# Scatter with the one-hot block as the stationary operand, in four 32-column groups

## What is computed

```python
h = relu(layernorm(x));  s = h[:, :32] @ W_up_s;  v = h[:, 32:] (as 32 x 3) @ W_up_v
w0, w1, w2, w3 = split(silu(silu(edge_feats @ A1 + b1) @ A2 + b2) @ A3, 4)
out_s0 = s[src] * y_s * w0            # y_s, y_v: columns 0 and 1..3 of edge_attr_4
out_s3 = sum_i v[src]_i * y_v_i / sqrt(3) * w3
out_v1 = s[src] * y_v * w1            # 3 components
out_v2 = v[src] * y_s * w2            # 3 components
message = segment_sum([out_s0, out_s3, out_v1, out_v2], dst) / 10
out = x + [message_s @ W_out_s, message_v @ W_out_v]
```

## Time and profile before

| | |
|---|---|
| median of three runs, without the profiler | 2046.74 us (2044.48 to 2048.28) |
| span of the profiled execution | 2586.7 us |
| TensorE matmuls busy | 2104.9 us (81% of the span) |
| weight loads busy | 1617.6 us (63%) |
| GpSimd (gathers) busy | 1577.2 us (61%) |
| VectorE busy | 928.9 us (36%) |
| ScalarE busy | 397.6 us (15%) |
| mean granted TensorE clock | 0.792 |
| DMA | 128.17 MB, mean 50 GB/s |

### The profile page before, as it was taken

One profiled execution on the slowest core, in us unless ns is written; L12 is line 12 of the kernel. 1 busy time (PEld: TensorE's weight loads), 2 busy tenths in 40 slices (PEclk: granted clock), 3 DMA queues, 4 the chain that ended last, 5 costly groups with the idle time before them and its releaser, 6 DMA issues.

```text
span 2586.7 us, 35524 instructions
## 1 busy us (share of the span) xinstructions
PE 2104.9 (81%) x10298; PEld 1617.6 (63%) x10298; DVE 928.9 (36%) x2228; ACT 397.6 (15%) x640; POOL 1577.2 (61%) x1627
## 2 busy tenths in 40 slices
PE   6477888878888889787878888888888878888878
PEld 4366666656666667566656666666666666666666
DVE  4233333333333333333333333333333334333334
ACT  3011111111111111111111111111111111111111
POOL 5666666566566566666666566656666656666661
PEclk8687788788778777877878788778788877778787
DMA  6111111111111111111111111111111111111111
GB/s 189 50 47 45 46 45 46 44 45 47 43 47 46 43 45 45 47 45 45 45 47 45 45 46 46 44 44 46 46 44 46 46 45 43 47 45 47 46 47 62
DMA packets 111056, 128.17 MB, mean 50 GB/s; under 512 B 70594, under 2 KB 83170, under 8 KB 110916
## 3 DMA queue, kind: packets, MB, share of 16 engines
q0 software_dynamic: 50336, 102.64, 15.2%
q1 hardware_dynamic: 60516, 25.37, 3.8%
q10 hardware_dynamic: 192, 0.02, 0.0%
HBM read 121.47 MB, written 6.43 MB: 49 GB/s over the span
## 4 chain that ended last, share of the span: by engine, by line
PE 62%; another core or an unknown queue 19%; issue 15%; ACT 2%; DVE 0%; ACTq 0%; DVEq 0%; DMA 0%; SPq 0%
PE pss L703 25%; PE psw L687 14%; PE pso L715 8%; PE ps L670 7%; PE ps L677 7%; ACT sums L542 1%; ACT h L524 1%; ACT h L529 0%; DVE msgs L613 0%; ACTq L541 0%; DVEq L621 0%; DMA ef_in<-in_efT 0%; ACTq L557 0%; SPq L453 0%
## 5 line engine op out<-in xcount | busy, mean ns | idle before, releaser
L498 POOL DMA_INDIRECT rows<-node_table,src_in x1563 | 1560.3, 998 | 943.5 <-DVE msgs L613 469.5
L703 PEld LDWEIGHTS pss<-onehot,msgs 128*128 128x128 f32 x6256 | 895.0, 217 | 554.8 <-issue 513.8
L703 PE MATMUL pss<-onehot,msgs 128*128 128x32 f32 (+1 forms) x6256 | 947.9, 301 | 246.8 <-issue 233.6
L611 DVE TENSOR_TENSOR msgs<-rows,psw 128x256 f32<-128x256 f32 x391 | 164.7, 421 | 1583.4 <-remote 905.3
L687 PE MATMUL psw<-a_bd,h 128*128 128x256 f32 x1564 | 527.9, 470 | 22.8 <-issue 11.7
L715 PE MATMUL pso<-sums,w_out 128*128 128x128 f32 x1568 | 282.5, 338 | 171.2 <-ACT sums L542 144.8
L687 PEld LDWEIGHTS psw<-a_bd,h 128*128 128x128 f32 x1564 | 339.2, 240 | 69.2 <-issue 21.7
L613 DVE TENSOR_TENSOR msgs<-rows,psw 128x768 f32<-128x768 f32 x391 | 370.6, 948 | 0.0
L715 PEld LDWEIGHTS pso<-sums,w_out 128*128 128x128 f32 x1568 | 251.9, 244 | 189.2 <-issue 187.7
L670 PE MATMUL ps<-ef_in,a_bd 16*128 16x512 f32 x392 | 257.6, 740 | 19.8 <-DMA ef_in<-in_efT 10.9
L524 ACT ACTIVATE h<-ps,b_sb 128x512 f32<-128x512 f32 x196 | 134.9, 688 | 824.9 <-remote 398.5
(11 more groups left out here) (55 smaller groups left out, 88.0 us busy)
## 6 DMA issues: line engine op xcount, KB each, us to landing
rows<-node_table,src_in POOLq DMA_INDIRECT x1563
ef_in<-in_efT SPq DMA_DIRECT2D x98, 64.0 KB
xT_sb<-in_xT SPq DMA_DIRECT2D x7, 448.0 KB, 8.3
x_sb<-in_x SPq DMA_DIRECT2D x7, 448.0 KB, 7.8
attr_in<-in_attr SPq DMA_DIRECT2D x98, 32.0 KB
out_T<-xT_sb SPq DMA_DIRECT2D x1, 3136.0 KB, 8.8
node_table<-tab_sb SPq DMA_DIRECT2D x7, 256.0 KB, 3.7
src_in<-in_src SPq DMA_DIRECT2D x98, 8.0 KB
```

The lines of the kernel that those rows point to most:

```text
L498: pool.indirect_dma_start(out=rows[:, QT * p + t, :], out_offset=None, in_=table, in_offset=bass.IndirectOffsetOnAxis(ap=src_in[:, b, at:a ...
L611: dve.tensor_tensor(m[:, :, :, 0, :], g[:, :, 0, :].unsqueeze(2).broadcast_to([P, QT, 2, MUL]), w[:, :, :, 0, :], ALU.mult)
L703: last = nc.tensor.matmul(pss[:, o % 2, 2 * q + i, c0:c1, :].rearrange("p c w -> p (c w)"), msgs[:, p % SLOTS, t, part, :], onehot[:, g % ...
```

## The change

`scatter` swaps its operands. The one-hot block of one tile and one attribute (128 edges x 32 nodes) is now stationary, and the messages are moved past it: 128 columns for attribute 0, twice 32 columns for each of attributes 1 to 3. Its output is 32 partitions (nodes) by 256 columns (features). The four tiles of a quad belong to four different windows, and each writes its own 32 partitions of `pss`. The host reorders the edges so that a quad holds one tile of each of four windows, and the next quad the other tile of each.

The sums of an oct then lie as 128 nodes x 256 features. `copy_sums` copies 256 columns instead of 512; a new step `turn` transposes them in two matmuls against an identity; a new ScalarE step `copy_turned` brings 256 columns back to SBUF; `project` needs two matmuls instead of four. `msgs` and `onehot` have four slots instead of two. `layer_1` and `layer_2` stand one per quad, two octs ahead. Windows are added six behind instead of eight. In the last pass all eight quads run (seven before), still with 27 gathers.

```diff
+OW = QT
+MSG_SLOTS = 4
+HOT_SLOTS = 4
-WINDOW_LAG = 2 * OW
+WINDOW_LAG = OW + 2
-OUT_WEIGHT_LOADS = 1 + 3 * 3
+OUT_WEIGHT_LOADS = 2 + 3 * 2
...
-        pss = pb("pss", [P, 2, OW, 4, W])
-        pso = pb("pso", [P, 2, 512])
+        pss = pb("pss", [P, 2, 512])
+        psx = pb("psx", [P, 2, 512])
+        pst = psx[:, 0, 0:CH]
+        pso = psx[:, 1, 0:OW * W]
...
+                pool.memset(identity[:, :], 0.0).then_inc(identity_built, 1)
+                pool.wait_ge(identity_built, 1)
+                pool.affine_select(out=identity[:, :], in_=identity[:, :], compare_op=ALU.not_equal, fill=1.0,
+                                   base=0, pattern=[[-1, P]], channel_multiplier=1).then_inc(identity_built, 1)
...
+                    def copy_sums(j, o):
+
+                        act.wait_ge(scatter_done, j * QB + 2 * o + 2 + SCATTER_CREDIT)
+                        act.wait_ge(sums_turned, j * OCTS + o + 1)
+                        act.activation(sums[:, o % 2, :], pss[:, o % 2, 0:CH], ACT.Copy).then_inc(sums_copied, 1)
+
+                    def copy_turned(j, o):
+
+                        act.wait_ge(sums_turned, j * OCTS + o + 1 + TURN_CREDIT)
                         act.wait_ge(out_ready, j * OCTS + o + 1)
+                        act.activation(sums_t[:, o % 2], pst.rearrange("p (k n) -> p k n", k=2),
+                                       ACT.Copy).then_inc(turned_copied, 1)
...
-                        for i in range(2):
-                            for part, c0, c1 in ((0, 0, 1), (1, 1, 4)):
-                                for t in (2 * i, 2 * i + 1):
-                                    last = nc.tensor.matmul(
-                                        pss[:, o % 2, 2 * q + i, c0:c1, :].rearrange("p c w -> p (c w)"),
-                                        msgs[:, p % SLOTS, t, part, :],
-                                        onehot[:, g % 2, QT * k + t, c0:c1, :].rearrange("p c w -> p (c w)"),
-                                        start=(t == 2 * i), stop=(t == 2 * i + 1))
+                        for c in range(4):
+                            for w in range(OW):
+                                m = msgs[:, p % MSG_SLOTS, w]
+                                acc = pss[W * w:W * (w + 1), o % 2, 0:CH]
+                                if c == 0:
+                                    moving, to = m[:, 0, :], acc[:, 0:F]
+                                else:
+                                    moving = m[:, 1, :].rearrange("p (k u) -> p k u", k=4)[:, 0:c + 1:c, :]
+                                    to = acc.rearrange("p (k u) -> p k u", k=8)[:, 3 + c:8:4 - c, :]
+                                last = nc.tensor.matmul(to, onehot[:, o, QT * half + w, c, :], moving,
+                                                        start=(half == 0 and c == 0), stop=(half == 1 and c == 3),
+                                                        skip_group_check=True)
                         last.then_inc(scatter_done, 1)
...
+                    def turn(j, o):
...
+                        for k in range(2):
+                            last = nc.tensor.transpose(pst[:, k * P:(k + 1) * P], sums[:, o % 2, k * P:(k + 1) * P],
+                                                       identity[:, :])
+                        last.then_inc(sums_turned, 1)
...
+                        for k in range(2):
+                            last = nc.tensor.matmul(pso, w_out[:, k, :], sums_t[:, o % 2, k, :],
+                                                    start=(k == 0), stop=(k == 1))
                         last.then_inc(out_ready, 1)
```

More of the change, by code:

```diff
@@ L78, in quad_tiles @@
 def quad_tiles(p):
-    return max(0, min(QT, LAST_TILES - QT * p))
+    o, half = divmod(p, 2)
+    begins = [o * OCT_EDGES + w * GROUP + half * P for w in range(OW)]
+    return sum(b < LAST_EDGES for b in begins)
 def gnn_layer_kernel(nc, x, xT, src, dst, dst_groups, attr, efT, Wus, Wuv, A1, b1, A2, b2, A3, Wos, Wov, outT):
@@ L554, in _ @@
-                    for part in range(4):
-                        silu(0, 0, part)
+                        for o in range(OCTS):
+                            ahead = (j, o + 2) if o + 2 < OCTS else (j + 1, o + 2 - OCTS)
+                            before = not (first and o == 0)
+                            if before:
+                                copy_sums(j, o - 1)
+                            if not (last and o + 2 >= OCTS):
+                                silu_1(*ahead)
+                            if before:
+                                copy_turned(j, o - 1)
+                            if not (last and o + 2 >= OCTS):
+                                silu_2(*ahead)
@@ L723, in iteration @@
                     def iteration(j, first=False, last=False):
-                        quads = LAST_QUADS if last else QB
-                        for p in range(quads):
-                            b, k = divmod(p, QUADS)
-                            if p + 1 < quads:
+                        for p in range(QB):
+                            o, half = divmod(p, 2)
+                            ahead = (j, o + 2) if o + 2 < OCTS else (j + 1, o + 2 - OCTS)
+                            if p + 1 < QB:
@@ L730, in iteration @@
                                 layer_3(j + 1, 0)
-                            if b == 0:
-                                mlp_part(j, 1, k)
-                            elif not last:
-                                mlp_part(j + 1, 0, k)
-                            ends = last and p == quads - 1
-                            if not ends:
-                                scatter(j, p)
-                            if p % 2 == 0 and not (first and p == 0):
-                                project(j, p // 2 - 1)
-                            if ends:
-                                scatter(j, p)
-                    for part in range(4):
-                        mlp_part(0, 0, part)
+                            if half == 1 and not (first and o == 0):
+                                project(j, o - 1)
+                            if not (last and o + 2 >= OCTS):
+                                (layer_1, layer_2)[half](*ahead)
+                            if half == 0 and not (first and o == 0):
+                                turn(j, o - 1)
+                            scatter(j, p)
+                    for o in range(2):
+                        layer_1(0, o)
+                    for o in range(2):
+                        layer_2(0, o)
                     layer_3(0, 0)
```

149 lines of the change are left out of this document (72 added, 77 removed).

## The result

Six runs of each kernel side by side gave a median of 2041.42 us after the change (2039.56 to 2045.56) against 2047.51 us before: ratio 0.9972, 95% interval 0.9961 to 0.9982. The forecast was no change, 2048.3 us.

What follows compares the result with a forecast made beforehand. The prediction took GpSimd's gathers as the bound before and after. Prologue -0.4 and tail +2.0, all other terms 0, gave +1.6 us on the median of 2046.7: 2048.3 us, range 2020 to 2090.

Steps and rivals of the forecast that it cites:

- the floor of 2016 us: Whole kernel: 1563 gathers starting every 1.25 us plus 19.5 us behind the last start; lengthened gathers add up to 80 us.
- That the stalls belong to profiling: TensorE in the profiled execution: idle stretches between matmuls, inferred from some 540 us of span existing only under the profiler.
- TensorE's room: TensorE per quad: 3.94 us of work against 5.00 us for four gathers, so 1.06 us to spare.
- messages start when gathers land: VectorE: one-hot multiplications keep their place against the gathers, lengthening keeps its size; value 0, bounds -30 and +50 us.
- rival B: Gathers: TensorE delays them in the metric too and a shorter scatter frees them; about 2020 us, chance 0.11.
- The tail, "+2.0 us": Last messages to store: scatter +0.3, turn +0.8, copy_turned +0.4, project -0.4, four windows instead of two +0.9; together +2.0 us.
- The 19.5 us of the floor: End of the kernel: time from the last gather's start through messages, scatter, projection, window and store to the span's end.
- Scatter, 2.15 us: TensorE, new scatter per quad: column groups one after the other, loads hidden, 2.15 us; bounds 0.54 and 3.55 us.
- estimate of 2.0 us from sequencer time: TensorE, new scatter: about 62 ns of sequencer time per MATMUL, counted on 32 pairs, 2.0 us per quad.
- Transposes: TensorE, projection: two transposes and two matmuls make 8 pairs per oct if a transpose splits like a product, again 0.92 us.
- Prologue, -0.4 us: Start of the kernel: two fewer w_out loads, up to -0.8 us, and two small GpSimd operations for the identity; taken as -0.4.
- Rival C: One-hot multiplication shifts against the gathers: 0.05 us in each of 196 octs is 10 us, 2038 or 2058 us; chance 0.13.

Runs made afterwards that it cites:

- the second profile: The kernel before, unchanged, profiled again: span 2046.5 us, in an execution that took 2048.32 us.
- after_layer3_twice: The kernel after with each layer_3 matmul issued twice, the second writing the same result: median 2045.64 us, ratio 0.9999 to the kernel before.
- after_one_group: The kernel after with all four windows of a quad written to partitions 0 to 31, one column group, sums wrong: 2041.63 us, ratio 0.9997 to the kernel before.
- before_four_slots: The kernel before with four slots of msgs and onehot instead of two, nothing else: ratio 0.9998 to the kernel before.
- before_half_scatter: The kernel before with the second tile of each window left out of the scatter, half the edges missing: median 2039.44 us, ratio 0.997.

## Why the prediction was wrong, point by point

**The bound: right.** The gathers bound both kernels, and the floor of 2016 us with up to 80 us of lengthened gathers on top describes both: the traces hold 1503.5 and 1500.0 us of gather work, of which 1563 x 0.944 = 1475 is the undisturbed pace, so 28 and 25 us of lengthening.

**"That the stalls belong to profiling": wrong.** They belonged to one execution; the second profile has no such stretch. I had marked this step as an inference. It cost nothing in the sum, since I left the stalls out of the metric, but with them I left out TensorE altogether.

**What failed: TensorE's room was reckoned at full clock only.** That took two terms of the sum with it. The forecast was +1.6 us and the two traces are 5.9 us apart the other way; of these 7.5 us, 3.5 lie in the gathers (forecast 0), 4.5 in the tail (forecast +2.0, measured -2.5), and 0.5 go the other way in the prologue.

**VectorE, "messages start when gathers land", value 0: failed.** It holds for 353 of 391 quads before, and for 384 of 392 after. I had compared TensorE's 3.94 us at full clock with 5.00 us and called the difference room. But half-clock stretches remain without the stalls (granted clock 0.50 from 180 to 190 us), and there the work of a quad takes nearly twice as long. In before, 22 of the 196 multiplications follow messages that had waited for TensorE, and the gathers beside these 22 carry 8.4 of the 28 us of lengthening; after has six such multiplications and 1.4 of 25 us. The lengthened gathers came out 3.5 us cheaper in all, not 0. That is rival B's cause (TensorE delays gathers in the metric too), with one difference. The gathers never wait for messages; they are lengthened. B priced all 30 us above the floor, 2020 us. Most of those 30 us come from the usual distance of 0.98 us, which the change doesn't touch: the gathers beside the other 174 multiplications carry 20 us. That late messages are the way holds for these two kernels; `after_layer3_twice` and `after_one_group` lose the gain by other ways (above).

**The tail, "+2.0 us": wrong in sign.** It measured -2.5 us (22.9 to 20.4 behind the start of the last gather). From the last messages to the store it was 10.8 us before and 7.6 after, not 2 us more. The 19.5 us of the floor were taken at full clock as well; they measured 22.9. I laid the new steps end to end behind the last messages and took all at full clock. In both traces part of the tail runs at half clock (granted clock 0.50 from 2028 to 2036 us before, and from 2016 to 2024 us after), and TensorE still has the scatter of the last quad but one and a projection to do when the last messages come. TensorE's tail before and after:

```profile
2024.92 2.03 PE L703 MATMUL pss<-onehot,msgs 128*128 128x32 f32 x16 [1.88 <-DVE msgs L613]
2027.64 2.04 PE L715 MATMUL pso<-sums,w_out 128*128 128x128 f32 x8 [0.69 <-ACT sums L542]
2029.47 3.57 PE L703 MATMUL pss<-onehot,msgs 128*128 128x32 f32 x16
2033.51 1.97 PE L715 MATMUL pso<-sums,w_out 128*128 128x64 f32 x8 [0.47 <-ACT sums L542]
```
```profile
2020.32 1.29 PE L736 MATMUL pss<-msgs,onehot 128*32 128x128 f32 x32 [0.79 <-DVE msgs L640]
2021.54 2.08 PE L714 MATMUL psw<-a_bd,h 128*128 128x256 f32 x4
2023.41 0.64 PE L746 MATMUL psx<-identity,sums 128*128 128x128 f32 x2
2023.97 1.12 PE L736 MATMUL pss<-msgs,onehot 128*32 128x128 f32 x32
2025.02 0.71 PE L755 MATMUL psx<-sums_t,w_out 128*128 128x128 f32 x4
2025.66 0.76 PE L736 MATMUL pss<-msgs,onehot 128*32 128x128 f32 x32
2026.92 0.44 PE L746 MATMUL psx<-identity,sums 128*128 128x128 f32 x2 [0.50 <-ACT sums L556]
2027.84 0.71 PE L755 MATMUL psx<-sums_t,w_out 128*128 128x128 f32 x4 [0.47 <-ACT sums_t L562]
```

The last scatter took 3.57 us before and 0.76 after, the last projection 1.97 and 0.71. `turn` took 0.5 us of the 0.8 given, `copy_turned` the 0.4. Something I had overlooked works against the gain: in the kernel after the last three tiles lie in two quads, where before they lay in one, so that there is one more pass of messages and scatter, and the last messages start 3.55 us behind the start of the last gather, against 2.87 before.

How much the tail gives hangs on where a half-clock stretch falls. `before_four_slots` has the last scatter at half clock too, 3.57 us, and 22.6 us of tail. In the two profiles of the kernel before with the multiplication first it took 1.92 and 2.02 us, and the tails are 19.9 and 19.5 us, no longer than the 19.5 to 20.4 of after and its variant with the same edit. So the 2.5 us belong to the lower clock as much as to the shorter scatter.

**Scatter, 2.15 us: the wrong end of the bounds.** It takes 0.6 to 0.8 us at full clock, close to the low bound of 0.54. The 2.15 us was right for the case that it described: one column group measured 2.24 to 2.33. The drain that the Trainium skill's "TensorEngine Tiling (Array Packing)", section Key Properties, names for a change of mode does not stand out: from the last narrow load at 1504.77 + 0.60 to the loads of `layer_3` at 1505.60 it is 0.23 us, against 0.17 to 0.24 us of idle time ahead of other groups of loads. The Trainium skill's same page and section say that different tiles can load weights and multiply in parallel; 0.83 against 2.33 us agrees with that. The prediction's estimate of 2.0 us from sequencer time left out a condition: the Trainium skill's "TensorE: Matmul & The Clock Gate", Part 1, has the 62 ns only with hardware decoding off. Here the loads of 32 pairs stand within 0.60 us, 19 ns each.

**Transposes:** the two transposes of an oct left two records, 0.44 us, so a transpose does not split like a product; `turn` and `project` together have 6 pairs per oct, not 8.

**Prologue, -0.4 us:** the first gather came at 45.0 before and 45.1 after, and between 43.4 and 45.9 in the other traces. No effect can be told from that spread.

**Rival C** (a shift of the multiplication) did not decide between these two kernels: it starts 1.30 us after the messages in both. Its price was right, though: at 10 us for each 0.05 us it says 20 us for the 0.1 us that gave 16, and 62 us for the 0.31 us later that left the kernel 57 us behind before on that chip.

## What to carry to other kernels

Take a second profile before building on the stalls of a first one, above all when its span and the unprofiled time differ by more than the runs do. When an engine off the critical path has room only at its full clock, ask what it does at the lower one, and what its lateness moves: here, in before, it moved a VectorE instruction against GpSimd's issue. Look for every way in which it can be late: messages, window additions and the end of the kernel each showed in one of these traces. In a kernel bound by the issue of indirect DMAs, look at what stands beside each gather; moving one VectorE instruction by 0.1 us gained 16 us, more than twice what the new scatter gained.

## What the runs showed of the hardware that I had not expected

- A gather started less than 1.10 us after the one-hot multiplication (1.22 us, two SBUF inputs) ends at 2.04 us after its start, 0.82 us after its end; later ones take 0.94 us. The shorter `equal` (0.42 us, two SBUF inputs) has the same 0.82 us behind it.
- 32 pairs with 32-column weights in four column groups take 0.60 us of loads, 19 ns per pair, where a pair with 128-column weights took 111.
- The mean granted clock differed between kernels whose times differ by less than 0.4%: 0.992 (`after_one_group`, matmuls busy for 94% of the span), 0.893 (before, 92%), 0.953 (`after_layer3_twice`, 83%), 0.813 (`before_half_scatter`, 82%), 0.846 (after, 76%). The order is not that of the busy share, so the clock of a changed kernel could not have been read off from its load.
- What stays open: why the first profiled execution stalled; how the 6 us split between late messages and tail in the mean of many executions, since each trace shows one; and what lengthens most of the long gathers of `after_layer3_twice`.
